# Accumulating stores onto x1 in the output, ScalarE sharing the eviction, and a statistics stream spread over sixteen turns

## The reference

```python
# layer 0: group norm, int8-quantised 3x3 convolution
x = x + _L0_conv_ref(_gn(x), L0_conv_weight, L0_conv_bias)
    # x_q = clip(round(x / 0.05)); w_q = clip(round(w / 0.01)); acc = conv3x3(x_q, w_q)
    # clip(round((acc * 0.0005 + bias) / 0.1)) * 0.1
# layer 1: group norm, then a depthwise 5x5 convolution whose filters are its own pooled input
x = x + _L1_conv_ref(_gn(x), L1_conv_conv_w, L1_conv_conv_b)
    # feat = conv_w (1x1) applied to x, + conv_b
    # filt = adaptive average pool of feat to 5 x 5, one filter per image and channel
    # out  = depthwise 5x5 convolution of feat with filt
```

## Time and profile before

| | |
|---|---|
| median of three runs | 6187.13 us |
| the profiled execution, its time | 6187.55 us |
| its span, first to last instruction | 6185.9 us |
| VectorE busy | 5284.7 us (85%) |
| TensorE busy (matmuls) | 4916.9 us (79%) |
| ScalarE busy | 3360.9 us (54%) |
| POOL busy | 889.3 us (14%) |
| transfers | 1615.46 MB, mean 261 GB/s |
| read from / written to memory | 1068.55 / 538.84 MB |

### The profile page before, as it was taken

One profiled execution on the slowest core, in us unless ns is written; L12 is line 12 of the kernel. 1 busy time (PEld: TensorE's weight loads), 2 busy tenths in 40 slices (PEclk: granted clock), 3 DMA queues, 4 the chain that ended last, 5 costly groups with the idle time before them and its releaser, 6 DMA issues.

```text
span 6185.9 us, 112158 instructions
## 1 busy us (share of the span) xinstructions
PE 4916.9 (79%) x43630; PEld 3222.5 (52%) x43798; DVE 5284.7 (85%) x5934; ACT 3360.9 (54%) x2005; POOL 889.3 (14%) x1444
## 2 busy tenths in 40 slices
PE   1767676767676779349989989989899899899899
PEld 0111111111111112138878878878788788788787
DVE  6787878787878787659989989989899899899898
ACT  1656565646564649235545545545455455455454
POOL 0000000000000001102212212112112121122122
PEclk9888788878888889679999999999999999999999
DMA  8999999999999999389999999999999999999998
GB/s 259 301 280 307 287 300 287 303 286 294 299 301 298 297 286 299 100 182 257 244 251 251 250 252 252 251 249 257 246 260 243 256 255 250 256 249 251 252 255 195
DMA packets 617611, 1615.46 MB, mean 261 GB/s; under 512 B 81338, under 2 KB 82618, under 8 KB 580282
## 3 DMA queue, kind: packets, MB, share of 16 engines
q1 hardware_dynamic: 239298, 640.73, 41.7%
q0 software_dynamic: 162240, 537.03, 27.1%
q10 hardware_dynamic: 215488, 429.94, 25.8%
HBM read 1068.55 MB, written 538.84 MB: 260 GB/s over the span
## 4 chain that ended last, share of the span: by engine, by line
DVE 43%; issue 7%; DMA 3%; PE 2%; ACTq 1%; POOL 0%; SPq 0%; ACT 0%; DVEq 0%; another core or an unknown queue 0%; POOLq 0%
DVE c_z L1003 16%; DVE c_xr L1039 16%; DVE c_feat L1029 12%; DMA c_xr<-x_scratch 3%; PE c_tps L1083 1%; ACTq L859 1%; PE c_cps L1063 0%; POOL c_feat L922 0%; SPq L887 0%; PE c_cps L1065 0%; PE c_cps L1064 0%; ACT c_z L969 0%; DVEq L1002 0%; SPq L872 0%
## 5 line engine op out<-in xcount | busy, mean ns | idle before, releaser
L1083 PE MATMUL c_tps<-c_feat,c_tt 123*128 123x256 f16 (+1 forms) x20736 | 2377.0, 273 | 13.8 <-DVE c_xr L1039 10.7
L1083 PEld LDWEIGHTS c_tps<-c_feat,c_tt 123*128 123x128 f16 (+1 forms) x20736 | 1992.1, 97 | 275.0 <-issue 15.6
L987 ACT ACTIVATE c_feat<-c_cps 122x1024 f16<-122x1024 f32 x576 | 822.5, 1428 | 1352.1 <-PE c_cps L1065 1352.1
L1039 DVE SCALAR_TENSOR_TENSOR c_xr<-c_tps,c_xr 57x1024 f32<-57x1024 f32 (+1 forms) x1152 | 1403.2, 1218 | 158.6 <-DMA c_xr<-x_scratch 125.7
L443 PE MATMUL b_ps<-b_xq,w0main 128*128 128x512 bf16 x2904 | 918.4, 419 | 656.9 <-ACT b_q L401 484.5
L969 ACT ACTIVATE c_z<-c_x,c_rs 128x976 f16<-128x976 f32 x576 | 1156.6, 2008 | 275.5 <-PE c_tps L1083 169.1
L1003 DVE SCALAR_TENSOR_TENSOR c_z<-c_x,c_rs,c_z 128x976 f16<-128x976 f32 x576 | 1087.1, 1887 | 105.3 <-ACT c_z L969 92.9
L1063 PE MATMUL c_cps<-w_high,c_z 128*128 128x128 f16 x4608 | 822.1, 222 | 421.5 <-DVE c_z L1003 385.6
L936 POOL DMA_DIRECT2D out_dram<-c_xr x1152 | 667.4, 580 | 2892.5 <-DVE c_xr L1039 2827.9
L401 ACT ACTIVATE b_q<-b_ps,q_bias 128x1024 int8<-128x1024 f32 x512 | 549.2, 1115 | 813.8 <-DVE b_x L521 745.5
L456 PE MATMUL b_ps<-b_xq,w0edge 64*32 64x512 bf16 x3048 | 931.3, 416 | 0.0
(11 more groups left out here) (129 smaller groups left out, 2267.0 us busy)
## 6 DMA issues: line engine op xcount, KB each, us to landing
x_scratch<-b_x POOLq DMA_DIRECT2D x256, 1024.0 KB, 12.3
c_xr<-x_scratch SPq DMA_DIRECT2D x576, 384.0 KB
out_dram<-c_xr POOLq DMA_DIRECT2D x576, 384.0 KB, 7.9
b_stream<-in_x_dram SPq DMA_DIRECT2D x672, 256.0 KB, 12.4
b_x<-in_x_dram ACTq DMA_DIRECT2D x276, 512.0 KB, 13.6
b_x<-in_x_dram SPq DMA_DIRECT2D x276, 512.0 KB, 11.7
c_tt<-table_scratch SPq DMA_DIRECT2D x64, 576.0 KB
c_xr<-x_scratch SPq DMA_DIRECT2D x512, 72.0 KB
```

What stands on the lines that cost most here:

```text
L987: act.activation(dst, cps[0:MAIN, s % 2, :, :].rearrange("p j (q o) -> p o q j", q=Q), ACT.Identity).then_inc(fh_done, 1)
L1039: last = dve.scalar_tensor_tensor(res, tps[PR * h:PR * h + n, s % 2, :, :], 1.0 / FS, res, ALU.mult, ALU.add)
L1083: last = pe.matmul(tps[:, s % 2, o % 4, :], tt[0:rows, o, tp, 2 * d:2 * d + 2, :].rearrange("k w m -> k (w m)"), feat[0:rows, (e * N + i) ...
```

## The change

It has three parts.

1. **x1 lives in the output.** The scratch tensor is gone: POOL stores x1 to `out` in its own layout (image, channel, row, column), four transfers of 32 partitions per chunk instead of two of 128. In the second stage the final stores add to what is there (`accum_op=ALU.add`), so the loads of `c_xr` are dropped; `c_xr` has four slots instead of six, and VectorE and ScalarE wait for a slot's store themselves. x1 blocks are loaded from `out` by SyncE at step 6, in four transfers of 32 partitions (partitions are now (column quarter, channel), so `rstd_cq` and a spread copy of the weights drop out). Before it stores rows of block j - 1, POOL waits until block j, which overlaps it, is loaded.
2. **ScalarE shares the eviction.** VectorE's two additions become one scaled copy of the even columns; ScalarE makes the odd columns. `c_z` has four slots and ScalarE converts two steps ahead.
3. **The statistics' stream.** Eight of the twelve streamed chunks of image b + 1 are taken in turns 0, 1, 3, 4, 6, 7, 9, 10 of image b (`LATE_AT`); the other four (`EARLY`) are taken in turns 12 to 15 of image b - 1 into a tile of their own (for image 1 before image 0). `vector_variance` and `new_scales` move to turn N - 2, before the statistics of that chunk. The waits after each small reduction at an image's end become one.

```diff
-        for j in range(RESIDENT):
-            TAKEN[N - X_SLOTS + 3 + j].append(j)
+        LATE = STREAMED - EARLY
+        LATE_AT = {n * (N - EARLY) // LATE: n for n in range(LATE)}
+        EARLY_AT = {N - EARLY + k: k for k in range(EARLY)}
+        RESIDENT_AT = {N - X_SLOTS + 3 + j: j for j in range(RESIDENT)}
...
+                    if more and n in LATE_AT:
+                        load_stream(sp, next_x, b, b + 1, EARLY + LATE_AT[n])
+                    if early and n in EARLY_AT:
+                        load_stream(sp, after_x, b, b + 2, EARLY_AT[n])
+
+            for k in range(EARLY):
+                load_stream(sp, next_x, 0, 1, k)
...
                     if more and n == N - 2:
                         gs.vector_spread(dve, b + 1, mv_x)
-                    if more and n == N - 1:
+                        gs.vector_variance(dve, b + 1)
                         new_scales(b + 1)
...
-                    for h in range(2):
-                        rows = slice(JB // 2 * h, JB // 2 * (h + 1))
-                        pool.dma_start(x1v[b, n, :, rows, :], xt[:, s, rows, :]).then_inc(x1_stored[s], 16)
+                    for r in range(Q):
+                        pool.dma_start(x1v[b, n, r, :, :, :], xt[C * r:C * r + C, s, :, :]).then_inc(x1_stored[s], 16)
...
-            eng.dma_start(xt[:, x_slot(e, j), lo:hi, :],
-                          x1v[2 * p + e + de, :, r0 + lo:r0 + hi, :]).then_inc(x1_loaded[x_slot(e, j)], 16)
+            for q in range(Q):
+                eng.dma_start(xt[C * q:C * q + C, x_slot(e, j), lo:hi, :],
+                              x1v[e + de::2][p, q, :, r0 + lo:r0 + hi, :]).then_inc(x1_loaded[x_slot(e, j)], 16)
...
                 if not banded:
+                    load_x1(sp, p, e, 0)
+                    load_x1(sp, p, e, 1)
                     for g in range(4):
                         load_table(p, e, g)
                 for s in range(STEPS):
-                    if banded:
-                        load_xr(p, e, j - 1, s)
...
+                    if s == 6 and pointwise and (j + 2 < N or another(p, e)):
+                        load_x1(sp, p, e, j + 2)
...
-                    pool.wait_ge(summed, count(p, e, TILES, m + 1) + START)
+                    pool.wait_ge(odd_out, count(p, e, TILES, m + 1) + START)
+                    pool.wait_ge(even_out, count(p, e, TILES, m + 1) + START)
                     for lo, hi in ((0, SPLIT), (SPLIT, n)):
                         pool.dma_start(out[e::2][p, 4 * s:4 * s + 4, r0 + lo:r0 + hi, :].rearrange("c h w -> h c w"),
-                                       xr_rows(m, lo, hi)).then_inc(stored[m % XR_SLOTS], 16)
+                                       xr_rows(m, lo, hi), accum_op=ALU.add).then_inc(stored[m % XR_SLOTS], 16)
...
+                    if banded:
+                        m = STEPS * (j - 1) + s
+                        wait_slot(act, p, e, m)
+                        act.wait_ge(band_done, count(p, e, TILES, m + 1) + START)
+                        res, conv = half_out(m, rows_out(j - 1), 1)
+                        act.activation(res, conv, ACT.Identity, scale=1.0 / FS).then_inc(odd_out, 1)
...
-                        dve.wait_ge(xr_loaded[m % XR_SLOTS], count(p, e, TILES // XR_SLOTS * 32, (m // XR_SLOTS + 1) * 32) + START)
-                        for h in range(2):
-
-                            res = xr_rows(m, 0, n).rearrange("h c (j p) -> h p c j", p=2)[:, 1 - h, :, :]
-                            last = dve.scalar_tensor_tensor(res, tps[PR * h:PR * h + n, s % 2, :, :], 1.0 / FS,
-                                                            res, ALU.mult, ALU.add)
-                        last.then_inc(summed, 1)
+                        res, conv = half_out(m, rows_out(j - 1), 0)
+                        dve.tensor_scalar(res, conv, 1.0 / FS, None, ALU.mult).then_inc(even_out, 1)
```

More of the change, by code:

```diff
@@ L474, in _, with take, take_stream @@
             last.then_inc(padded, 1)
-            TAIL = 2 + 2 * NSEG + 1
-            def take(tile, n, j0, rows):
+            TAIL = 4
+            def take(tile, into, n, j0, rows):
                 for j in range(rows):
-                    last = dve.bn_stats(st_x[:, n * JB + j0 + j, :], tile[:, j, :])
+                    last = dve.bn_stats(into[:, n * JB + j0 + j, :], tile[:, j, :])
                 return last
+            def take_stream(t, k, into, n):
+                for h in range(2):
+                    dve.wait_ge(stream_loaded[h], (nth_stream(t, k) + 1) * LOAD + START)
+                    take(xs[:, h, :, :], into, n, JB // 2 * h, JB // 2).then_inc(stream_read[h], 1)
             def means(t):
@@ L564, in _ @@
             new_scales(0)
-            with dve.Fori(0, nb - 1) as b:
-                body(b, True)
-            body(nb - 1, False)
+            for k in range(EARLY):
+                take_stream(1, k, st_early, k)
+            with dve.Fori(0, nb - 2) as b:
+                body(b, True, True)
+            body(nb - 2, True, False)
+            body(nb - 1, False, False)
         @block.gpsimd
@@ L747, in _ @@
         def _(sp):
-            for q in range(Q):
-                sp.dma_start(rstd_cq[q::Q, :], rstd[0:C, :]).then_inc(stored, 16)
             sp.wait_ge(tables_ready, 1)
@@ L759, in _, with depthwise @@
             sp.dma_start(table_d[nb, 0:1, 0:PR], blank[:, :]).then_inc(stored, 16)
-            sp.wait_ge(stored, 16 * (5 * lots + 1 + Q))
-def depthwise(nc, nb, k, x1, rstd, table_d, bias_d, out):
+            sp.wait_ge(stored, 16 * (5 * lots + 1))
+def depthwise(nc, nb, k, rstd, table_d, bias_d, out):
     with ExitStack() as ctx:
@@ L988, in group @@
-                if j + 2 < N or another(p, e):
-                    load_x1(act, p, e, j + 2)
-            act.wait_ge(cleared, 1 + START)
-            group(0, 0, 0, True, False)
-            for p in range(PAIRS):
-                for e in range(2):
-                    for j in range(1, N + 1):
-                        group(p, e, j, p < PAIRS - 1 or e == 0 or j < N, True)
+                    if pointwise:
+                        act.wait_ge(conv_done, count(p, e, TILES, STEPS * j + s + 1) + START)
+                        dst = feat[0:MAIN, (e * N + j) % 2, 0, :, 1:FP - 1].rearrange("p o (q j) -> p o q j", q=Q)[:, :, :, 8 * s:8 * s + 8]
+                        act.activation(dst, cps[0:MAIN, s % 2, :, :].rearrange("p j (q o) -> p o q j", q=Q), ACT.Identity).then_inc(fh_done, 1)
+                        nxt = ahead(p, e, j, s + 2)
+                        if nxt is not None:
+                            high(p, e, *nxt)
@@ L1060, in pointwise @@
                 for c in range(8):
-                    zh, zl = (z[:, s % 2, t, c, :] for t in range(2))
+                    zh, zl = (z[:, s % Z_SLOTS, t, c, :] for t in range(2))
                     dst = cps[:, s % 2, c, :]
```

159 lines of the change are left out of this document (77 added, 82 removed).

## The result

The changed kernel takes 6024.80 us (median of four runs, 6018.61 to 6033.23) beside 6186.79 for the kernel before (6175.35 to 6190.99): a ratio of **0.974** (0.972 to 0.976). It is faster, inside the range, but the gain is 162 us where 357 were forecast. The profiled execution took 6033.23 us with a span of 6031.5; one core, as before.

What follows compares the result with a forecast made beforehand. The prediction took VectorE to bound the second stage, with TensorE close behind, and transfers most of the first. From 6187.55 us, -204 - 70 - 53 - 30 = -357 gave 5830 us, range 5680 to 6090.

Steps and rivals of the forecast that it cites:

- The steps (-204): Second stage: 568 steps go from VectorE's 5.66 us to TensorE's 5.30 us, saving 204 us.
- Rival 4: Second stage: ScalarE binds if its half eviction takes over 1.85 us; at 2.01, 5.5 us a step, 5945 us; chance 0.04.
- The store (3.2 us a step): Second stage: the accumulating store takes double a plain store's 1.61 us of DMA engine time, 3.2 us a step.
- Rival 3: Second stage: accumulating store costs over 2.5 times a plain one, slower than before; at 3 times 6630 us; chance 0.12.
- The x1 load (2.02 us a step): Second stage: x1 loads keep their DMA engine time of 2.02 us a step; a 4.0 MB block alone takes 19 us.
- The boundary (-70): Second stage, between images: the stall falls from 28.1 to 17 to 18 us, seven times, -70 us (-160 to 0).
- rival 1: Second stage: the DMA engines bind mildly, likely 5.6 us a step, +170, 6000 us; chance 0.22.
- The start of the second stage (-53): Between the stages: x1 loads come before the tables, so first conversions start sooner, -53 us (-30 to -60).
- The first stage (-30): First stage: spread stream and narrower stores net -4 us an image, -30 us over seven (-110 to +200).
- 8 x 19.7 + 3 x 13 = 197 us for 217: First stage, turns 0 to 10: eight turns with a streamed chunk at 19.7 us, three without at 13, -20 an image.
- 16 + 2 - 5 = 13 us: First stage, image's end: +16 for early chunks' statistics, +2 waiting for earlier scales, -5 for the next image's sooner start.
- Rival 2 (stores, +200): First stage: narrow or wide-pitched stores slow transfer-bound turns from 19.7 to 22.5 us, +200, 6030 us; chance 0.12.

Runs made afterwards that it cites:

- The kernels on the boundary: Changed kernel with x1 block behind table group 2: 6005.6 us; behind all groups: 5965.5, with plain store too: 5871.3; half of each x1 load left out: 5919.9.
- the bunched kernel: Changed kernel with the eight late streamed chunks in turns 0 to 7 and none in turns 8 to 11: 5956.1 us, ratio 0.962 to the kernel before.
- the last kernel: Changed kernel with late streamed chunks in turns 0 to 7 and the x1 block behind all four table groups at an image's end: 5865.7 us, ratio 0.948.

## Why the prediction was right or wrong

Against the forecast the first stage is off by 107 us, the boundaries by 115, the start of the second stage by 6 and by 23 that it didn't have; the steps gained 46 us more than it said.

**The steps (-204): right in kind, too small.** Measured -250. TensorE is busy 150.00 of 150 us, and the banded passes start 5.29 us apart. The old step was 5.73 us and not 5.66: the 5.74 us to which VectorE's four rows add was the step, and the "overlap of neighbours" was a miscount of steps. The evictions cost what their nearest rows said, 1.22 and 1.11 us. Four slots of c_xr suffice mid-image. Rival 4 is out.

**The store (3.2 us a step): right in kind, too high.** 0.510 x 5.29 = 2.70 us. Rival 3 (over 2.5 times) is out at 1.67 to 1.8.

**The x1 load (2.02 us a step): wrong, too low.** 0.508 x 5.29 = 2.69 us. The two errors nearly cancel, 5.39 for 5.22 without tables; that the sum still fitted beside TensorE was luck. The forecast looked at partitions and not at the pieces. A partition got 512 bytes of a row before, too, but the other quarters of that row lay right behind in memory and went in the same transfer, and the packets were of 2034 bytes. A transfer of one column quarter has only 512 bytes in a row, and its packets are of that size. The forecast took 4.0 MB in 19 us alone; alone (2702 to 2732 us) the queue gets this:

```profile
DMA packets 10206, 5.18 MB, mean 173 GB/s; under 512 B 80, under 2 KB 10206, under 8 KB 10206
```

which makes 23 us, at a DMA share of 1.13, and SyncE can issue nothing else for most of that. The Trainium skill (DMA: Bandwidth & Descriptors, Specifications) has line rate from 512 bytes on. By that the smaller pieces would be free; the trace disagrees: 173 GB/s into 32 partitions at a time, where the earlier trace rows has 210 in larger packets into as many.

**The boundary (-70): wrong, +45.** The step that failed is "about 9 of the load's 19 us get done; ... 17 to 18 us". The mechanism, group 1 behind x1 in SyncE's queue, is the one in the trace, and the order alone is worth 10.5 us. Measured are 29.4 us for those 17 to 18, against an old boundary of 23.0 and not 28.1. Two sizes were off: the load needs 23 us alone, and the forecast let group 1 (its 4 us) follow at the full rate of an idle stage; SyncE issued it in 8.14 us and it landed 15.56 us later. The kernels on the boundary and the one with the plain store show that the addition (6.6), the order (10.5) and the x1 bytes (15.3) each hold a part; they overlap, so their sum says nothing. This is rival 1 in the one place where it came true: the DMA engines bind at the boundary (share 1.18 while TensorE stands), not in the steps.

**The start of the second stage (-53): right at -47, and then +23 that no step had.** The third x1 block is issued behind two blocks and four table groups, its issues take 34 + 7 us, and ScalarE waits for it. The forecast followed this start only to the first banded matmul.

**The first stage (-30): wrong, +77.** The step that failed is "8 x 19.7 + 3 x 13 = 197 us for 217". Where it had -20 us, turns 0 to 11 took 232.1 us for 234.0. Two of three turns take 11 to 16 us by ScalarE's rows, even quicker than said, but the third takes 30 to 34: three together stay at what three full turns took. The 19.7 us was a mean over two phases, 220 and 410 GB/s, and the change altered their mix. When the empty turns stand in a row (the bunched kernel), turns with a stream take 20.7 us on average by the same rows and the four without 14.0, near the forecast's two prices, and the period is 311.9, or 310.1 in the last kernel, for the 309.3 that -4 an image had meant. So the prices hold for a stream in a row, and the change does not have one. The terms of the last turns, 16 + 2 - 5 = 13 us, were right: they measured 13.5.

**Rival 2 (stores, +200): not as priced.** Narrow stores alone cost nothing (310.0). With the output's layout and the old stream the period is 317.2, so the layout may cost up to 4 to 7 us an image, a fifth of the rival's price. It rests on the period of one profile of each kernel, and in the spread stream it doesn't show (323.1 with the layout, 325.8 without); it stays open.

## What to carry to other kernels

A mean rate of the DMA engines holds for one mix of queues and directions; before work is taken out of some turns, look at the rate in slices, for the phases of which the mean is made. Count the steps of a window by two engines' instructions: half a step too many in 300 us hid some 40 us of the gain here. When a tensor moves to another layout, count the bytes that lie in a row for one transfer, and look for what else the issuing queue must issue meanwhile. And where a step moves in an in-order queue, cost both orders: here the one left in place was worth 10 us an image, the cheapest gain of the case.

## What the hardware showed that was not expected

- An accumulating store costs 1.67 times a plain one per MB (3.98 for 2.38% of the engines), and 1.8 times (4.37%) with half of the x1 loads gone. Its packets are smaller (12.80 MB in 7893, for 11.97 MB in 4082), and POOL's issue of one takes 1054 ns on average, while the median landing, 7.9 us, is that of before.
- Issuing loads of 32 partitions in 512-byte pieces (0.98 MB each) holds the issuing engine, the later ones of a block more than the first: of the four issues of a block on SyncE the first takes 0.3 us at the median, the others 4.6, 8.5 and 8.1, together 21.6 us, near the block's own 23 us alone. With half of x1 left out the two issues take 0.3 and 4.3 us. ScalarE's issue of a whole block took 0.70 us before.
- The DMA share read 1.18 at the boundary, in 512-byte and table packets together, and 1.13 with 512-byte packets alone, though no window shown of the kernel before is above 1.06; the rates were 214 and 173 GB/s. A share over 1 is no measure of work done.
